# Repeated identity products on TensorE ahead of eight of its waits, in a fused attention and mixture-of-experts layer

## The chip, the cores and the metric

One core of one Trainium2 chip runs the whole layer in one launch. The metric is the device time of a launch in microseconds (us), the median of several. One more execution was taken with the hardware profiler; all rows below are from it, and their times count from the start of its span.

## The reference

The layer takes x of 4 batches by 512 tokens by 512 features and does the following, cut to what matters here:

```
mod = (silu(c) @ wmod) in six parts: sa, ca, ga, sb, cb, gb
h   = layernorm(x) * (1 + ca) + sa
q, k, v = h @ Wq + bq, h @ Wk + bk, h @ Wv + bv     (16 heads of 128)
w   = softmax(q k / sqrt(128) + causal mask)
x   = x + ga * ((w v) @ Wo + bo)
h   = layernorm(x) * (1 + cb) + sb
x   = x + gb * (sum over the top 2 of 8 experts of weight * swiglu(h) + shared swiglu(h))
```

An expert has 352 hidden features; the shared one has 704 and is run as two experts of 352.

## The kernel before

Every large product is made three times: each operand is split into a high part and a low remainder (`_hi`, `_lo`), and `mm3` (L1112) issues hi*hi, hi*lo and lo*hi into one PSUM bank. ScalarE (ACT) copies out of PSUM into the high part, VectorE (DVE) subtracts it to get the low part, and TensorE (PE) waits for that. Each engine has its own program; they are tied by semaphores, and the order within an engine is the order in which the code is written.

**Stage 1** makes q for all batches and heads. TensorE first multiplies out two parts of `mod`, transposes the first batch's normalised x (`transposes`, L1142, called from L1157) and then waits in `q_rows` (L1163) until the modulated rows are split (`hlo_ok`). The banks in use are 2 to 7; bank 1 is first written by the second head.

**Stage 2** is attention, 32 steps of one pair of heads and one batch (`step` in the TensorE program, driven by `walk_steps`). A step multiplies `scores(0)` to `scores(5)` (three parts for each of the two heads, banks 2 and 3), puts the output projection of the step before between them (`project(0)` to `project(3)`), makes the values (`values(0)` to `values(3)`, banks 0 and 1), transposes the softmax blocks (`turn`) and multiplies them with the values (`weigh(0)` into bank 6, `weigh(1)` into bank 7). `scores(i)` waits for the exponentials of part i-2. `weigh(h)` takes three groups g of transposed blocks, each behind a wait for its low part (L1272). The first step has no projection and has all its values first (L1294); the last step (`last`) has no keys for a next step, and does `turn(0)`, `turn(1)`, `weigh(0)`, `weigh(1)` at its end. In the last step DVE's program runs, between the low part of head 0's output (`o_part(0)`) and the low parts of head 1's transposed blocks, the four `c_stats` of a layer norm; ACT copies head 1's blocks only after `weigh(0)` is done.

**Stage 3** is the feed-forward part, 71 jobs of one tile of 128 tokens each (`job`, L1374): 16 jobs of the first shared half, 6 of the second, 39 routed slots and then 10 more of the second shared half. A job multiplies the gate half (`half(..., 0)`), transposes the previous job's hidden rows (`turn_mid`), multiplies the up half (`half(..., 1)`), transposes the next job's tokens (`turn_rows`, which waits for their load) and multiplies the previous job's down projection (`down`). Job 0 comes without a previous one. Between job 0 and job 1 stands a wait for the down weights (L1405), between job 15 and job 16 one for the second shared expert (L1412), job 21 (`R0 - 1`) transposes the first gathered tokens, and the last `down` (L1474) follows its `turn_mid` (L1473).

`ident` (the 128x128 identity) and `causal` (the additive mask block) are in SBUF from the start of the kernel to its end, both of four-byte floats. The `causal` block is added by DVE in `maxima`.

Of the kernel before, what the change touches and what calls it, by code (L numbers as in the profile page):

```python
# [30 lines left out]
P = 128  # L31
# [24 lines left out]
R0 = NT + NB1  # L56
# [70 lines left out]
def adaln_layer(nc, x, wq, bq, wk, bk, wv, bv, wo, bo, gate_t, wexp, c_t, wmod, ident_in, causal_in,  # L127
                tri_in, coef_in, out):
    ctx = ExitStack()
    with ctx:  # L130
# [18 lines left out]
        bank = [ctx.enter_context(nc.psum_tensor(f"bank{i}", [P, T], F32)) for i in range(8)]  # L149


        ident = sbuf(ctx, "ident", [P, P])
        causal = sbuf(ctx, "causal", [P, P])
# [958 lines left out]
        def _(pe):  # L1112
            def mm3(dst, terms):
# [5 lines left out]
                        k += 1  # L1119
                return ins  # L1120

            pe.wait_ge(silu_c, 1)

            def mod_piece(m):
# [10 lines left out]
            def transposes(b, i):  # L1135

                pe.wait_ge(xn_ok, b * TT + (i + 1))
                if not (isinstance(b, int) and b == 0):
                    pe.wait_ge(hf_ok, b * TT + (i - 1))
                for c in range(DC):  # L1140
                    dst = bank[2 + i if isinstance(b, int) and b == 0 else 4 + i % 2]
                    ins = pe.transpose(dst[:, c * P:(c + 1) * P], x_in[:, i, c * P:(c + 1) * P],  # L1142
                                       ident[:, :])
                ins.then_inc(tx_full, 1)
# [10 lines left out]
            ins.then_inc(modt_full, 1)  # L1155
            for i in range(1, TT):
                transposes(0, i)  # L1157

            def q_rows(b, more, first):
                def hidden(h, c):  # L1160
# [53 lines left out]
            def step(p, b, first, last):  # L1214
                n = p * B + b

                def scores(i):

                    h, rows = i // 3, S_PARTS[i % 3]
                    if i % 3 == 0:  # L1220
                        pe.wait_ge(k_ok, n * 2 + (h + 1))
                        pe.wait_ge(q_ok, n * 2 + (h + 1))
                    if not (first and i < 2):
                        pe.wait_ge(s_exp, n * 6 + (i - 1))
                    for r in rows:
                        w = (r + 1) * P
                        at = ROW_AT[r] - ROW_AT[rows[0]]
                        dst = bank[2 + i % 2][:, at:at + w]
                        for k, (a, m) in enumerate(((q_hi, k_hi), (q_hi, k_lo), (q_lo, k_hi))):
                            ins = pe.matmul(dst, a[:, h, r * P:w], m[:, h, 0:w], start=(k == 0), stop=(k == 2))  # L1230
                    ins.then_inc(s_full, 1)

                def values(t):

                    g, i = t // 2, t % 2
                    if i == 0:
                        pe.wait_ge(wv_ok, p + 1)
                        if not first:
                            pe.wait_ge(wo_add, n * TT + (g - 1))
                        else:  # L1240
                            pe.wait_ge(k_ok, g + 1)
                    rows = slice(t * P, (t + 1) * P)
                    ins = mm3(bank[g][:, i * 2 * P:(i + 1) * 2 * P],
                              [(h_hi[:, b * DC + c, rows], h_lo[:, b * DC + c, rows], wv_hi[:, c, :], wv_lo[:, c, :])
                               for c in range(DC)])
                    if i == 1:
                        ins.then_inc(v_full, 1)

                def turn(h, groups):

                    if groups[0] == 0:
                        pe.wait_ge(p_ok, n * 6 + (3 * h + 3))
                    for g in groups:
                        blocks = PT_GROUPS[g]
                        if last and h == 1:
                            if g == 2:
                                pe.wait_ge(v_ok, n * 2 + 1)
                        elif not (first and h == 0 and g < 2):
                            pe.wait_ge(pt_ok, n * 6 + (3 * h + (1 if g == 2 else 0)))
                        for k, at in blocks:  # L1260
                            for r in range(k, TT):
                                ins = pe.transpose(  # L1262
                                    bank[pt_bank(h, g, last)][:, at + (r - k) * P:at + (r - k + 1) * P],
                                    prob[:, h, ROW_AT[r] + k * P:ROW_AT[r] + (k + 1) * P], ident[:, :])
                        ins.then_inc(pt_full, 1)

                def weigh(h):

                    if not first:
                        pe.wait_ge(o_ok, n * 2 + (h - 1))  # L1270
                    for g, blocks in enumerate(PT_GROUPS):
                        pe.wait_ge(pt_ok, n * 6 + (3 * h + g + 1))  # L1272
                        pe.wait_ge(v_ok, n * 2 + (1 if g == 0 else 2))
                        for k, at in blocks:
                            w = (TT - k) * P
                            cols = slice(PT_AT[g] + at, PT_AT[g] + at + w)
                            vals = slice(h * P, (h + 1) * P)
                            for q, (a, m) in enumerate(((v_hi, pt_hi), (v_hi, pt_lo), (v_lo, pt_hi))):
                                ins = pe.matmul(bank[6 + h][:, k * P:T], a[:, k, vals], m[:, cols],  # L1279
                                                start=(k == 0 and q == 0), stop=(g == 2 and q == 2))  # L1280
                    ins.then_inc(o_full, 1)

                def project(i):
                    if not first:
                        free = [(k_ok, n * 2 + 1), (k_ok, n * 2 + 2), (wo_add, n * TT - 3), (wo_add, n * TT - 2)][i]
                        out_tile(n - 1, p if b > 0 else p - 1, i, free)

                def next_keys(h, chunks):
                    if not last:
                        keys(n + 1, p if b < B - 1 else p + 1, (b + 1) % B, h, chunks)  # L1290

                if first:
                    for t in range(TT):
                        values(t)  # L1294
                scores(0)
                scores(1)
                project(0)
                project(1)
                scores(2)
                project(2)  # L1300
                scores(3)
                project(3)
                if not first:
                    values(0)
                scores(4)
                if not first:
                    values(1)
                scores(5)
                if not first:
                    values(2)  # L1310
                    values(3)
                turn(0, (0, 1))
                if last:
                    turn(0, (2,))
                    turn(1, (0, 1, 2))
                    weigh(0)
                    weigh(1)
                    return
                next_keys(0, range(DC))
                turn(0, (2,))  # L1320
                next_keys(1, (0,))
                weigh(0)
                turn(1, (0, 1))
                next_keys(1, range(1, DC - 1))
                turn(1, (2,))
                weigh(1)
                next_keys(1, (DC - 1,))
# [46 lines left out]
            def job(n, s, wofs, prev_ofs, route=False, prev=True, nxt=True, free=None, up_ld=None, prev_at=WD,  # L1374
                    gathered=False):
                half(n, s, wofs, 0, route)
                if up_ld:
                    pe.wait_ge(*up_ld)
                if prev:
                    turn_mid(n - 1, 1 - s)  # L1380
                half(n, s, wofs, 1, route)
                if nxt:
                    turn_rows(n + 1, 1 - s, loaded(n + 1, 1 - s, gathered))
                if prev:
                    down(n - 1, 1 - s, prev_ofs, free, prev_at)
# [16 lines left out]
            pe.wait_ge(g_ok, 1)  # L1402
            pe.wait_ge(we_ld[0], 32)
            job(0, 0, 0, 0, route=True, prev=False, up_ld=(we_ld[1], 32))
            pe.wait_ge(we_ld[2], 32)  # L1405
            job(1, 1, 0, 0, route=True, prev_at=WDA)
            job(2, 0, 0, 0, route=True, prev_at=WDA)
            job(3, 1, 0, 0, route=True, free=(y_gb, 1), prev_at=WDA)
            with pe.Fori(2, NT // 2) as j:
                for k in range(2):  # L1410
                    job(j * 2 + k, k, 0, 0, route=True, free=(y_gb, j * 2 + (k - 2)), prev_at=WDA)
            pe.wait_ge(w_ld[1], 32)  # L1412

            def slot_tokens(c):
# [55 lines left out]
            for n in range(Z0 + 1, NJ):  # L1470
                k = n - Z0
                job(n, n % 2, 0, 0, nxt=n + 1 < NJ, free=(y_ev, NSLOT + k - 2) if k < 3 else (y_gb, R0 + k - 2))
            turn_mid(NJ - 1, (NJ - 1) % 2)  # L1473
            down(NJ - 1, (NJ - 1) % 2, 0, (y_gb, R0 + NB2 - 2))  # L1474


# [648 lines left out]
```

## Time and profile before

| | us |
|---|---|
| median of three runs | 1673.3 |
| lowest, highest | 1672.33, 1673.81 |
| profiled execution, its own time | 1676.7 |
| its span, first to last instruction | 1674.9 |

TensorE is busy 1591.5 us of the span (95%), VectorE 891.5 (53%), ScalarE 697.0 (42%), GpSimd 591.2 (35%). The mean granted TensorE clock is 0.981 of full speed. "PE" is TensorE's multiplying, "PEld" its loading of the stationary operand, which lies beside it. A granted clock of 1.00 is 2.4 GHz and 0.50 is 1.2 GHz.

### The profile page before, as it was taken

To read this page: it belongs to the slowest core of one execution; us is meant where nothing else is said; L and a number is where in the kernel's file an instruction comes from. 1 tells how busy PE (TensorE), PEld (TensorE's weight loads), DVE (VectorE), ACT (ScalarE), POOL (GpSimd) and SP (SyncE) were. 2 spreads that over 40 slices of the span, in tenths; PEclk is the share of its full clock that TensorE was granted. 3 is DMA by queue.
4 is the path that set the end of the run, shared out by engine and by line. 5 is a ranking of instruction groups with operands and counts; after the bars stand their busy time and mean duration, and the time that the engine had idled before them with its cause. 6 is when DMAs were issued, how large, how long until landed. Compare 5 with 4: busy or idle time off the path is not lost.

```text
span 1674.9 us, 29946 instructions
## 1 busy us (share of the span) xinstructions
PE 1591.5 (95%) x9012; PEld 1382.1 (83%) x9013; DVE 891.5 (53%) x2091; ACT 697.0 (42%) x1689; POOL 591.2 (35%) x625
## 2 busy tenths in 40 slices
PE   6999989999999999999999999978998899999997
PEld 3888578888888888888888888767898798888886
DVE  4333136666666566656665666767656322222267
ACT  4222155555555555555555555432231232222332
POOL 0001024544554535444545455655211211111043
PEclk9999999999999999999999999989998999999998
DMA  7522225243343253432423442585213445655455
GB/s 262 200 101 106 95 72 164 64 123 116 111 122 103 72 153 96 129 109 78 152 72 107 118 125 66 164 318 193 88 38 132 151 182 182 252 205 192 178 182 176
DMA packets 178453, 232.40 MB, mean 139 GB/s; under 512 B 78600, under 2 KB 137352, under 8 KB 175328
## 3 DMA queue, kind: packets, MB, share of 16 engines
q1 hardware_dynamic: 168112, 204.74, 37.0%
q0 software_dynamic: 5680, 18.62, 3.9%
q10 hardware_dynamic: 4608, 8.39, 1.6%
q8 instruction: 27, 0.44, 0.1%
q14 instruction: 26, 0.21, 0.0%
HBM read 151.70 MB, written 80.00 MB: 138 GB/s over the span
## 4 chain that ended last, share of the span: by engine, by line
PE 79%; DVE 8%; DMA 6%; ACT 3%; issue 3%; SPq 1%; another core or an unknown queue 0%; POOL 0%; ACTq 0%; DVEq 0%; POOLq 0%
PE bank L1118 48%; PE bank L1195 9%; PE bank L1279 7%; PE bank L1230 7%; DMA slot_results<-y_sb 5%; PE bank L1262 4%; PE bank L1131 1%; PE bank L1336 1%; PE bank L1362 1%; DVE o_lo L1604 1%; DVE pt_lo L1602 1%; ACT prob L939 1%; DVE ht_lo L1778 1%; DMA q_transposed<-q_out 1%; ACT o_hi L972 1%
## 5 line engine op out<-in xcount | busy, mean ns | idle before, releaser
L1118 PE MATMUL bank<-w,xt_hi 128*128 (+2 forms) x1136 | 287.0, 335 | 9.9 <-issue 8.2
L939 ACT ACTIVATE prob<-bank,neg_max 128x128 f32<-128x128 f32 (+3 forms) x256 | 134.0, 526 | 241.3 <-DVE neg_max L1643 238.7
L1118 PEld LDWEIGHTS bank<-w,xt_hi 128*128 128x128 f32 x1136 | 198.7, 191 | 22.0 <-issue 15.5
L680 POOL CAST q_hi<-q_raw 128x512 fp32r<-128x512 f32 x64 | 71.2, 1112 | 386.2 <-PE bank L1230 238.2
L1118 PE MATMUL bank<-w,xt_lo 128*128 (+2 forms) x568 | 185.6, 327 | 0.0
L1118 PE MATMUL bank<-w,ht_hi 128*128 (+3 forms) x426 | 142.6, 416 | 19.2 <-DVE ht_lo L1778 19.2
L1778 DVE TENSOR_TENSOR ht_lo<-bank,ht_hi 128x128 fp32r<-128x128 f32 (+1 forms) x213 | 48.4, 283 | 195.8 <-ACT ht_hi L1052 192.0
L1118 PE MATMUL bank<-wv_hi,h_lo 128*128 128x256 f32 x512 | 144.7, 283 | 0.0
L1118 PE MATMUL bank<-wv_lo,h_hi 128*128 128x256 f32 x512 | 144.5, 282 | 0.0
L1118 PE MATMUL bank<-wv_hi,h_hi 128*128 128x256 f32 x512 | 144.3, 282 | 0.0
L951 ACT ACTIVATE prob<-prob,row_inv 128x128 f32<-128x128 f32 (+3 forms) x256 | 136.2, 556 | 1.4
L1638 DVE TENSOR_REDUCE row_max<-bank 128x1 f32<-128x128 f32 (+3 forms) x256 | 119.8, 489 | 6.6
L682 POOL TENSOR_TENSOR ch_lo<-ch_raw,ch_hi 128x340 fp32r<-128x340 f32 x128 | 117.9, 921 | 10.2
L1602 DVE TENSOR_TENSOR pt_lo<-bank,pt_hi 128x512 fp32r<-128x512 f32 (+1 forms) x192 | 108.4, 592 | 14.8 <-ACT pt_hi L965 14.8
L1604 DVE SCALAR_TENSOR_TENSOR o_lo<-bank,bv_c,o_hi 128x512 fp32r<-128x512 f32 x64 | 48.1, 751 | 116.9 <-ACT o_hi L972 116.9
L1195 PE MATMUL bank<-h_hi,wk_hi 128*128 128x512 f32 x256 | 109.0, 426 | 0.8 <-ACT q_out L900 0.8
L1118 PE MATMUL bank<-h_hi,wq_hi 128*128 128x512 f32 (+1 forms) x256 | 102.3, 400 | 6.9 <-DVE h_lo L1579 6.5
L1118 PEld LDWEIGHTS bank<-w,xt_lo 128*128 128x128 f32 x568 | 108.2, 191 | 0.0
L1602 DVE TENSOR_TENSOR v_lo<-bank,v_hi 128x512 fp32r<-128x512 f32 x64 | 44.3, 692 | 118.2 <-ACT v_hi L958 118.2
L965 ACT ACTIVATE pt_hi<-bank 128x512 fp32r<-128x512 f32 (+1 forms) x192 | 93.3, 525 | 33.2 <-PE bank L1262 32.5
L1118 PEld LDWEIGHTS bank<-w,ht_hi 128*128 128x128 f32 (+1 forms) x426 | 76.8, 193 | 35.9 <-DVE ht_lo L1778 16.8
L900 ACT ACTIVATE q_out<-bank,bq_c 128x512 f32<-128x512 f32 x64 | 43.9, 689 | 143.8 <-PE bank L1118 134.0
(203 smaller groups left out, 4081.6 us busy)
## 6 DMA issues: line engine op xcount, KB each, us to landing
ch_raw<-wexp SPq DMA_DIRECT2D x128, 170.0 KB, 2.6
experts_hi<-ch_hi SPq DMA_DIRECT2D x128, 170.0 KB, 2.0
experts_lo<-ch_lo SPq DMA_DIRECT2D x128, 170.0 KB, 2.1
w<-experts_hi SPq DMA_DIRECT2D x10, 2176.0 KB, 8.4
w<-experts_lo SPq DMA_DIRECT2D x10, 2176.0 KB, 15.0
q_transposed<-q_out SPq DMA_DIRECT2D x64, 256.0 KB, 2.0
q_raw<-q_transposed SPq DMA_DIRECT2D x32, 512.0 KB, 4.2
slot_results<-y_sb SPq DMA_DIRECT2D x39, 256.0 KB
```

Of the source, the lines that this page charges most:

```text
L680: pool.tensor_copy(hi, raw).then_inc(split_hi, 1)
L682: pool.tensor_tensor(lo, raw, hi.bitcast(F32), ALU.subtract).then_inc(done, 1)
L939: ins = act.activation(prob[:, h, ROW_AT[r]:ROW_AT[r] + (r + 1) * P], bank[2 + i % 2][:, at:at + (r + 1) * P], ACT.Exp, bias=neg_max[:, h, ...
L951: ins = act.activation(part, part, ACT.Copy, scale=row_inv[:, h, r:r + 1])
L965: act.activation(pt_hi[:, PT_AT[g]:PT_AT[g] + PT_LEN[g]], bank[pt_bank(h, g, last)][:, 0:PT_LEN[g]], ACT.Copy).then_inc(pt_hi_ok, 1)
L1118: ins = pe.matmul(dst, a, m, start=(k == 0), stop=(k == last))
L1195: ins = pe.matmul(bank[h][:, :], a[:, c, h * P:(h + 1) * P], m[:, b * DC + c, :], start=(c == 0 and k == 0), stop=(c == DC - 1 and k == 2))
L1230: ins = pe.matmul(dst, a[:, h, r * P:w], m[:, h, 0:w], start=(k == 0), stop=(k == 2))
L1262: ins = pe.transpose(bank[pt_bank(h, g, last)][:, at + (r - k) * P:at + (r - k + 1) * P], prob[:, h, ROW_AT[r] + k * P:ROW_AT[r] + (k + 1) ...
L1279: ins = pe.matmul(bank[6 + h][:, k * P:T], a[:, k, vals], m[:, cols], start=(k == 0 and q == 0), stop=(g == 2 and q == 2))
L1602: dve.tensor_tensor(dst, src, hi.bitcast(F32), ALU.subtract).then_inc(done, 1)
L1638: ins = dve.tensor_reduce(row_max[:, h, r:r + 1], bank[2 + i % 2][:, at:at + (r + 1) * P], AX_X, ALU.max)
```

## The change

A helper `spin(b, count)` on TensorE multiplies the identity (stationary) by the causal block (moving) `count` times into the first 128 columns of bank b. Nothing reads the result; it waits on nothing and signals nothing. It is called at eight places, here lettered in program order: A (10 times, before the first wait of `q_rows`), B (4 times, first attention step, between the values and `scores(0)`), C (6 times, last attention step, between `project(1)` and `scores(2)`), D (8 times, last attention step, inside `weigh(0)` before its third group), E (8 times, after job 0), F (6 times, before job 16), G (11 times, in job 21 before the transposes of the first gathered tokens) and H (6 times, before the last `down`).

```diff
@@ tensor program
+            def spin(b, count):
+                for _ in range(count):
+                    pe.matmul(bank[b][:, 0:P], ident[:, :], causal[:, :], start=True, stop=True)
...
             for i in range(1, TT):
                 transposes(0, i)
+            spin(1, 10)
...
                     for g, blocks in enumerate(PT_GROUPS):
+                        if last and h == 0 and g == 2:
+                            spin(1, 8)
                         pe.wait_ge(pt_ok, n * 6 + (3 * h + g + 1))
...
                 if first:
                     for t in range(TT):
                         values(t)
+                    spin(7, 4)
                 scores(0)
                 scores(1)
                 project(0)
                 project(1)
+                if last:
+                    spin(7, 6)
                 scores(2)
...
                 half(n, s, wofs, 1, route)
+                if isinstance(n, int) and n == R0 - 1:
+                    spin(2, 11)
                 if nxt:
                     turn_rows(n + 1, 1 - s, loaded(n + 1, 1 - s, gathered))
...
             job(0, 0, 0, 0, route=True, prev=False, up_ld=(we_ld[1], 32))
+            spin(4, 8)
             pe.wait_ge(we_ld[2], 32)
...
                     job(j * 2 + k, k, 0, 0, route=True, free=(y_gb, j * 2 + (k - 2)), prev_at=WDA)
+            spin(7, 6)
             pe.wait_ge(w_ld[1], 32)
...
             turn_mid(NJ - 1, (NJ - 1) % 2)
+            spin(0, 6)
             down(NJ - 1, (NJ - 1) % 2, 0, (y_gb, R0 + NB2 - 2))
```

## Rows read from the trace of the kernel before

**Rows 1.** The page: busy time of the engine; shares of the last-ending chain by engine.
```profile
PE 1591.5 (95%) x9012; PEld 1382.1 (83%) x9013; DVE 891.5 (53%) x2091; ACT 697.0 (42%) x1689; POOL 591.2 (35%) x625
...
PE 79%; DVE 8%; DMA 6%; ACT 3%; issue 3%; SPq 1%; another core or an unknown queue 0%; POOL 0%; ACTq 0%; DVEq 0%; POOLq 0%
```

**Rows 2.** Stretches: length, PE, PEld, DVE, ACT, POOL busy, clock, DMA share, GB/s.
```profile
20.61:27.06 6.45, 0.00 (x1) 0.01 (x1) 5.02 (x6) 6.45 (x16) 0.00 (x0) 0.71 0.71 253
27.06:30.10 3.04, 3.04 (x7) 2.46 (x8) 2.07 (x1) 3.04 (x3) 0.00 (x0) 0.50 0.16 60
238.19:248.56 10.37, 6.67 (x25) 5.15 (x25) 7.39 (x26) 7.44 (x22) 3.90 (x4) 0.67 0.22 51
1081.69:1088.24 6.55, 4.67 (x19) 4.12 (x19) 6.04 (x10) 1.07 (x2) 2.89 (x5) 0.74 0.83 249
1092.29:1095.97 3.68, 0.01 (x2) 0.00 (x1) 3.54 (x9) 0.96 (x5) 2.46 (x3) 0.88 1.04 390
1095.97:1101.90 5.93, 5.93 (x17) 4.97 (x18) 3.48 (x9) 2.71 (x7) 5.85 (x7) 0.50 0.49 145
1110.93:1116.59 5.66, 3.45 (x24) 3.12 (x24) 2.37 (x5) 2.73 (x6) 0.47 (x1) 1.00 0.96 333
1116.59:1121.25 4.66, 0.00 (x0) 0.03 (x1) 3.82 (x7) 2.05 (x4) 0.00 (x0) 0.75 1.05 409
1121.25:1125.78 4.53, 4.53 (x16) 4.04 (x16) 1.28 (x7) 0.57 (x1) 3.14 (x7) 0.50 1.03 418
1136.84:1140.97 4.13, 0.00 (x1) 0.03 (x1) 4.06 (x8) 0.60 (x1) 0.20 (x1) 0.81 0.88 312
1140.97:1146.26 5.29, 5.29 (x19) 5.20 (x20) 2.32 (x5) 1.14 (x5) 0.00 (x0) 0.50 1.07 388
1161.84:1168.20 6.36, 3.36 (x18) 2.96 (x18) 4.90 (x9) 0.60 (x1) 6.12 (x6) 1.00 0.16 44
1316.63:1322.84 6.21, 0.00 (x1) 0.00 (x1) 0.52 (x1) 0.00 (x0) 0.52 (x2) 0.80 1.05 447
1322.84:1327.16 4.32, 4.32 (x12) 3.55 (x13) 0.69 (x1) 0.60 (x1) 1.10 (x2) 0.50 0.86 329
1662.71:1666.06 3.35, 0.00 (x1) 0.00 (x0) 3.19 (x7) 0.60 (x3) 0.00 (x0) 0.86 0.17 64
1666.06:1670.30 4.24, 4.21 (x9) 2.81 (x9) 0.00 (x0) 0.00 (x0) 0.00 (x0) 0.50 0.03 12
```

**Rows 3.** Timeline of TensorE after job 16: start, length, engine, line, operation, operands, count.
```profile
1259.59 0.38 PE L1430 MATMUL bank<-hot,tri 128*128 128x128 f32 x2
1259.81 0.39 PE L1431 MATMUL bank<-hot,ones 128*128 128x128 f32 x2
```

**Rows 4.** Timeline around place D, from weigh(0)'s third group on; idle before in brackets.
```profile
1116.02 0.33 PE L1279 MATMUL bank<-pt_hi,v_hi 128*128 128x256 f32 x1
...
1116.71 0.69 ACT L972 ACTIVATE o_hi<-bank,bv_c 128x512 fp32r<-128x512 f32 x1 [2.71 <-PE bank L1279]
...
1117.43 0.75 DVE L1604 SCALAR_TENSOR_TENSOR o_lo<-bank,bv_c,o_hi 128x512 fp32r<-128x512 f32 x1 [2.98 <-ACT o_hi L972]
...
1118.10 2.46 DVE L1740 BATCH_NORM_STATS2 stat<-acc 128x6 f32<-128x512 f32 x4
1120.48 1.27 DVE L1602 TENSOR_TENSOR pt_lo<-bank,pt_hi 128x512 fp32r<-128x512 f32 x2
```

**Rows 5.** Stretches after place D, and the seven jobs before F, as in Rows 2.
```profile
1125.93:1140.97 15.04, 10.07 (x53) 8.89 (x53) 14.53 (x19) 3.12 (x5) 10.07 (x8) 0.95 0.62 239
...
1204.00:1251.60 47.60, 46.98 (x278) 43.69 (x278) 23.41 (x61) 15.54 (x46) 9.08 (x7) 1.00 0.16 47
```

**Rows 6.** Timeline around place B: last product of scores(0), then DVE's mask.
```profile
237.39 0.28 PE L1230 MATMUL bank<-k_hi,q_lo 128*128 128x256 f32 x1
...
238.26 0.42 DVE L1634 TENSOR_TENSOR bank<-bank,causal 128x256 f32<-128x256 f32 x1
```

**Rows 7.** Timeline around place F: the first product of job 16, and the next wait.
```profile
1251.59 0.49 PE L1118 MATMUL bank<-w,xt_hi 128*128 128x352 f32 x2
...
1257.40 0.73 PE L1118 MATMUL bank<-w,ht_hi 128*128 128x512 f32 x2 [0.98 <-DVE ht_lo L1778]
```

## The prediction

> **What bounds the kernel now.** I read the page's busy shares and the chain that ended last first: TensorE is busy 95% of the span and makes up 79% of the chain [rows 1]. So a product that is added on TensorE costs its full time unless it lies in one of TensorE's waits, and a product that is made faster gives its time back. I then went through the span for stretches in which the granted clock is below 1.00, and laid them beside TensorE's waits in the timeline. The clock goes to 0.50 nine times, each time after TensorE has waited, and comes back some microseconds after the work resumed. Eight of the nine stand in [rows 2]: those at places A to E, G and H, and the one from 1081.69 for comparison. While it is at 0.50 (1.2 GHz) TensorE is busy all the time in the rows after the waits (5.93 of 5.93 us, 5.29 of 5.29), so each microsecond at 0.50 has half a microsecond of loss in it. That is what the added products can win: work in a wait, so that the clock is not lowered.
>
> Added work in a wait keeps the clock up only if little of the wait is left. What little means has to come from this trace. The six waits of 3.35 us and more were all followed by 0.50. The ones between 1.8 and 3.1 us went both ways: the stretch from 1081.69 holds a wait of 6.55 - 4.67 = 1.88 us and fell, the one from 238.19 begins with 2.35 us and fell (10.37 - 6.67 = 3.70 us idle in all), the one from 1110.93 holds 5.66 - 3.45 = 2.21 and stayed at 1.00, the one from 1161.84 holds 6.36 - 3.36 = 3.00 and stayed at 1.00 [rows 2]. Two of four. So the length does not decide alone, and I give a wait cut down to 1.8 to 3.1 us an even chance of holding the clock, and a longer one none.
>
> The Trainium skill ("TensorE: Matmul & The Clock Gate", Part 1: The HAM clock gate) says that the moment at which the clock switches is not tied to the kernel and differs from run to run of the same code. By that rule a wait of middling length falls in some executions and not in others; the trace agrees in that 3.00 us stayed and 1.88 fell. The sum does not use it.
>
> **What one added product costs.** The kernel has the same form already, four-byte 128x128 by 128x128: L1430 and L1431 show two passes each, and start 1259.81 - 1259.59 = 0.22 us apart [rows 3]. So 0.22 us at full clock, and twice that, 0.44, at 0.50. 4, 6, 8, 10 and 11 of them are 0.88, 1.32, 1.76, 2.20 and 2.42 us; all 59 are 13.0 us of busy time.
>
> The skill's figure for a sustained stream of loads and products at 128 columns ("TensorE: Matmul & The Clock Gate", Back-to-back issue gap) is 81 ns. Were it that, ten would fill 0.8 us, less would be left hidden, and the three uncovered places below would cost 18 x 0.081 = 1.5 us at most. The row is for two passes of four-byte data and decides.
>
> **The places, one by one.**
>
> A (10). The wait from 20.61 is 6.45 us and hides 2.20; 4.25 are left, more than any wait that kept the clock. Cost 0, gain 0 (were the clock held, 3.04 / 2 = 1.5).
>
> G (11). The wait for the gathered tokens is 6.21 us and ends with a transfer, which TensorE doesn't move; 2.42 are hidden, 3.79 are left. Cost 0, gain 0 (at most 4.32 / 2 = 2.2) [rows 2].
>
> C (6). Wait 3.68, hidden 1.32, left 2.36. If the clock holds, 5.93 us at 0.50 become 2.97: gain 2.97, even chance.
>
> E (8). Wait 4.13, hidden 1.76, left 2.37. The wait belongs to DVE, busy 4.06 of it. Gain 5.29 / 2 = 2.65, even chance.
>
> H (6). Wait 3.35, hidden 1.32, left 2.03. The nine products of the last down projection take 4.24 us at 0.50; gain 2.12, even chance, and it is the end of the kernel, with nothing beside it [rows 2].
>
> B (4). There is no wait here: the products stand between the values and scores(0), and TensorE's wait of 2.35 us comes after scores(0) and scores(1). They push scores(0)'s end from 237.67 (237.39 + 0.28) to 238.55; DVE began its mask at 238.26, when it had done the values, so 0.88 turns into 0.3 us on the softmax chain, at most 0.88 [rows 6]. TensorE's wait after it shrinks by 0.5 to 1.8, but the stretch has 1.35 us more idle in two further waits for ACT, and is set by ACT and DVE; I take a gain of 0.3, bounds 0 and half of the time at 0.50 that TensorE works, about 2.7.
>
> D (8). No wait either: the third group of weigh(0) started at 1116.02 behind the second without a pause. Its end releases ACT's o_hi (idle 2.71 before it, for TensorE), that DVE's o_lo (idle 2.98, for ACT), then come the four statistics and pt_lo, for which weigh(1) waits until 1121.25 [rows 4]. All of this moves by 1.76, and TensorE's wait of 4.66 keeps its length, so the clock falls as before. Behind it DVE is busy 14.53 of the 15.04 us up to job 1, and from there TensorE nearly without a break (46.98 of 47.60) [rows 5]: nothing absorbs it. Cost 1.76; from below 1.2, if DVE's half microsecond of idle gives; from above 3.5, if it ran at 0.50. Gain 0 (at most 4.53 / 2 = 2.3, if the shifted wait happened to hold the clock).
>
> F (6). No wait: job 16 followed without a pause at 1251.59. But at 1257.40 TensorE waits 0.98 us for DVE, whose routing work doesn't depend on it. 1.32 - 0.98 = 0.34 are left, bounds 0.3 and 1.32 [rows 7]. No clock was lost here.
>
> **Sum.** Costs 0.3 + 1.76 + 0.34 = 2.4. Gains: half of (2.97 + 2.65 + 2.12) is 3.9, and 0.3 for B, 4.2. Since in other executions than the profiled one a wait of the kernel before may also have kept its clock, less is there to win on a median; I take 3.7. Net -1.3. The profiled execution took 1676.7 (span 1674.9 and 1.8 around it) and would come to 1675.4; it was 3.4 above the median of the runs, so on the median 1673.3 - 1.3 = 1672.0.
>
> **Rivals.** What a measurement of this kernel can tell from no change is about 0.2%, 3.35 us: faster is below 1669.95, slower above 1676.65.
>
> 1. The clock holds at C, E and H each time. For it: what is left is 2.03 to 2.37 us, under the 3.00 that held it. Against: 1.88 and 2.35 fell. Gain 7.74 less costs 2.4: -5.3, 1668.0; with a part at A or G 1666.
>
> 2. The clock falls everywhere all the same: the added products are hidden or paid for and don't do what they are there for, because whatever is left of the wait is enough. For it: the two that fell. The costs remain, +2.4, 1675.7, still within 0.2%.
>
> 3. Slower: the uncovered products at B, D and F are what decides. 18 x 0.22 = 3.96 us, if neither DVE's lead at B nor its lag at F takes a part, with no clock saved: 1677.3. It decides from the point at which more than 3.35 us of the 3.96 show and nothing is won at C, E and H. For it: three of eight places have no wait at all. Against: the cover at B and F can be read in the rows.
>
> **Chances.** Forecast (some hold, some fall) 0.45; rival 1 0.22; rival 2 0.20; rival 3 0.10; 0.03 for a gain beyond rival 1. Faster 0.22 + 0.03 = 0.25, slower 0.10, same 0.65. The forecast's own range is 1670 to 1674.5. The range that holds 8 in 10 reaches into rivals 1 and 2 to 1668.0 and 1676.2.
>
> **What would show it.** In the changed kernel's trace: the clock at 0.50 after A, D and G as before, a mix after C, E, H; weigh(0) to weigh(1) with the same wait of about 4.7 us but 1.8 later; the softmax wait after B shorter by 0.5; at F the wait of 0.98 gone. It would be wrong if a product of this form took much else than 0.22 us, if the clock held after A or G, or if the weights of D's successors were what job 1 waits for, so that D's delay vanished.

## The result, and the profile after

In its first measurement the changed kernel is slower. Over 20 runs of each on one chip its median is 1678.78 us and that of the kernel before 1674.97 (1670.16 to 1680.24); the ratio is 1.0026, 95% interval 1.0015 to 1.0037, so +4.4 us (+2.5 to +6.2). Two later measurements gave +0.7 and +1.8 us with zero inside the interval. The prediction was 1672.0, that is -1.3 us, no measurable change. The profiled execution took 1680.47 us, span 1678.6, against 1676.7 and 1674.9. The page of the changed kernel, busy time by engine, then the chain by engine:

```profile
PE 1604.9 (96%) x9130; PEld 1396.2 (83%) x9131; DVE 890.5 (53%) x2091; ACT 697.5 (42%) x1689; POOL 590.0 (35%) x625
...
PE 82%; DVE 7%; DMA 4%; ACT 3%; issue 3%; another core or an unknown queue 0%; SPq 0%; POOL 0%; ACTq 0%; DVEq 0%; POOLq 0%
```

TensorE has 118 more records, two for each of the 59 products, and 13.4 us more of busy time; 13.0 were forecast. DMA's and VectorE's shares of the chain go down [rows 1], as one would expect where parts of waits for them are now products. The mean granted clock rose only from 0.981 to 0.984.

The stretches of the changed kernel that answer to [rows 2], same columns (length, five engines' busy time, clock, DMA share, GB/s). In order, each wait with what follows it: A's, D's, E's, the one in job 3, the one for the gathered tokens, H's.

```profile
22.59:26.82 4.23, 0.00 (x1) 0.01 (x1) 2.78 (x5) 4.23 (x10) 0.00 (x0) 0.89 0.64 205
26.82:32.72 5.90, 5.90 (x14) 4.64 (x15) 4.93 (x3) 4.85 (x4) 0.00 (x0) 0.50 0.34 87
...
1114.82:1119.48 4.66, 0.00 (x1) 0.03 (x1) 3.83 (x7) 2.05 (x4) 0.00 (x0) 0.86 1.06 398
1119.48:1124.30 4.82, 4.71 (x16) 4.02 (x16) 1.42 (x8) 0.76 (x2) 3.43 (x7) 0.50 1.05 418
1138.47:1140.28 1.81, 0.01 (x2) 0.03 (x1) 1.81 (x4) 0.00 (x0) 0.00 (x0) 1.00 0.36 137
1140.28:1145.00 4.72, 4.72 (x32) 4.68 (x32) 3.16 (x8) 1.03 (x5) 0.00 (x0) 1.00 1.08 381
1158.74:1161.74 3.00, 0.00 (x1) 0.01 (x1) 2.96 (x6) 0.60 (x1) 3.00 (x3) 1.00 0.27 87
1161.74:1165.92 4.18, 4.18 (x12) 3.48 (x13) 1.56 (x3) 0.00 (x0) 2.96 (x3) 0.59 0.00 0
1318.17:1324.34 6.17, 0.00 (x0) 0.00 (x1) 0.52 (x1) 0.00 (x0) 0.51 (x2) 0.89 1.00 426
1324.34:1329.80 5.46, 5.46 (x16) 4.59 (x17) 0.69 (x1) 1.07 (x2) 1.10 (x2) 0.50 0.73 297
1669.68:1671.69 2.01, 0.00 (x1) 0.00 (x0) 1.92 (x5) 0.00 (x0) 0.00 (x0) 1.00 0.28 105
1671.69:1674.10 2.41, 2.35 (x9) 1.61 (x9) 0.02 (x1) 0.00 (x0) 0.00 (x0) 1.00 0.06 21
```

The rows to compare with before: E and H held the clock (1.00 after waits of 1.81 and 2.01 us), A and D did not, and two rows contradict what I wrote. The gathered-token wait is still 6.17 us long: the eleven products of G are not in it. And the 3.00 us in job 3, which kept the clock in [rows 2], were this time followed by 0.59, the mean of 4.18 us of which 3.4 stood at 0.50.

Where G's products stand, in the timeline of the changed kernel (start, length, engine, line, operation, count):

```profile
1299.84 0.49 PE L1372 MATMUL bank<-ident,h_mid 128*128 128x128 f32 x3
...
1302.11 2.62 PE L1124 MATMUL bank<-causal,ident 128*128 128x128 f32 x22
...
1304.56 0.60 PE L1346 MATMUL bank<-ident,xin 128*128 128x128 f32 x4
...
1324.34 0.90 PE L1346 MATMUL bank<-ident,xin 128*128 128x128 f32 x3 [6.17 <-DMA xin<-ffn_rows,slot_tokens]
```

And the same place in the kernel before, where the transposes of job 22's tokens start with no wait in front:

```profile
1302.84 0.33 PE L1118 MATMUL bank<-w,xt_lo 128*128 128x352 f32 x1
1303.01 0.60 PE L1336 MATMUL bank<-ident,xin 128*128 128x128 f32 x4
```

The wait of 6.21 us at 1316.63 in [rows 2] stands two jobs later, in job 23. In job 21 the 2.62 us are bare: nothing in the kernel waits there that they could hide in.

D went as forecast. The changed kernel around weigh(0)'s third group, columns as in [rows 4]:

```profile
1112.46 2.00 PE L1124 MATMUL bank<-causal,ident 128*128 128x128 f32 x16
1114.22 0.36 PE L1286 MATMUL bank<-pt_hi,v_hi 128*128 128x256 f32 x1
...
1114.93 0.69 ACT L972 ACTIVATE o_hi<-bank,bv_c 128x512 fp32r<-128x512 f32 x1 [5.81 <-PE bank L1286]
...
1115.65 0.75 DVE L1619 SCALAR_TENSOR_TENSOR o_lo<-bank,bv_c,o_hi 128x512 fp32r<-128x512 f32 x1 [6.07 <-ACT o_hi L972]
...
1119.48 0.77 PE L1286 MATMUL bank<-pt_hi,v_hi 128*128 128x512 f32 x1 [4.66 <-issue]
```

ACT's idle time ahead of o_hi grew from 2.71 to 5.81 us and DVE's from 2.98 to 6.07, while TensorE's own wait is 4.66 us as before: the products only moved it. Of the 3.1 us more, 1.8 are the products. Most of the rest is a stretch at 0.50 from 1107.9 to 1111.3, behind the wait of 2.2 us before the last block of turn(0), which in [rows 2] (from 1110.93) had kept the clock. No product was added there either.

### The profile page after: what moved, and what is told of

It reads as the page before. It is cut to its first block, busy times and chain, and to the rows that moved or that the text cites. A ratio compares the mean times of both kernels' runs of the same rounds, so it can differ in the third digit from the quotient of the medians.

```text
span 1678.6 us, 30182 instructions
## 1 busy us (share of the span) xinstructions
PE 1604.9 (96%) x9130; PEld 1396.2 (83%) x9131; DVE 890.5 (53%) x2091; ACT 697.5 (42%) x1689; POOL 590.0 (35%) x625
## 4 chain that ended last, share of the span: by engine, by line
PE 82%; DVE 7%; DMA 4%; ACT 3%; issue 3%; another core or an unknown queue 0%; SPq 0%; POOL 0%; ACTq 0%; DVEq 0%; POOLq 0%
PE bank L1118 50%; PE bank L1200 9%; PE bank L1286 7%; PE bank L1235 7%; PE bank L1267 4%; DMA slot_results<-y_sb 4%; PE bank L1135 1%; PE bank L1346 1%; PE bank L1372 1%; DVE pt_lo L1617 1%; DVE o_lo L1619 1%; ACT o_hi L972 1%; ACT prob L939 1%; DVE ht_lo L1793 1%; DVE row_max L1653 1%
## 5 line engine op out<-in xcount | busy, mean ns | idle before, releaser
L1118 PEld LDWEIGHTS bank<-w,ht_hi 128*128 128x128 f32 (+1 forms) x426 | 76.9, 194 | 33.0 <-DVE ht_lo L1793 13.6
```

The lines of the kernel that those rows point to most:

```text
L1118: ins = pe.matmul(dst, a, m, start=(k == 0), stop=(k == last))
```

## The experiments

All ratios are against the kernel before on the same chip in the same session. In the three sessions the kernel before had medians of 1670.09 (20 runs), 1673.26 (23) and 1670.54 us (23), with mean clocks of 0.983, 0.983 and 0.984. A difference in us is the ratio's, times the median of the kernel before; it can differ a little from the difference of the two medians. Diffs are against the changed kernel, if nothing else is said.

| kernel | session | median us | ratio, 95% | mean clock |
|---|---|---|---|---|
| changed kernel, first measurement | | 1678.78 | 1.0026, 1.0015 to 1.0037 | 0.985 |
| uncovered | 1 | 1674.85 | 1.0026, 1.0012 to 1.0040 | 0.984 |
| covered | 1 | 1665.24 | 0.9975, 0.9956 to 0.9994 | 0.988 |
| uncovered4 | 1 | 1692.63 | 1.0133, 1.0112 to 1.0155 | 0.986 |
| fill | 1 | 1658.99 | 0.9929, 0.9912 to 0.9946 | 0.998 |
| after_again (changed kernel) | 2 | 1672.96 | 1.0004, 0.9993 to 1.0016 | 0.988 |
| g_moved | 2 | 1673.12 | 0.9994, 0.9984 to 1.0005 | 0.987 |
| fill_half | 2 | 1665.04 | 0.9957, 0.9943 to 0.9972 | 0.993 |
| after_third (changed kernel) | 3 | 1671.62 | 1.0011, 0.9996 to 1.0027 | 0.987 |
| covered_again | 3 | 1667.88 | 0.9987, 0.9972 to 1.0002 | 0.986 |
| fill2 | 3 | 1659.14 | 0.9936, 0.9920 to 0.9951 | 0.998 |

My theory after the result: the uncovered products (B, D, F, and G as well) cost more than the covered ones (A, C, E, H) give. The rival: the costs are as predicted, and the covered ones cost something by themselves.

**uncovered**: B, D, F and G alone.

```diff
-            spin(1, 10)            # A; and C, E and H likewise
```

> Only B (4), D (8), F (6) and G (11). Theory 1 (the wait that G was meant for stands two jobs later, in job 23; at job 21 TensorE goes through without a pause, so G costs its full 11 x 0.215 us): B 0.3 + D 1.7 + F 0.3 + G 2.4 = +4.7 us over the kernel before, and the clock falls where it did. Theory 2 (G is hidden, as predicted): +2.4. Theory 3 (the slowdown isn't the products' own time but the routed stage, whose waits for slot_results stores happened to be longer): within 1 us of the kernel before.

Measured +4.3 us (+2.0 to +6.7). So these four by themselves make a loss of the size first measured for the whole.

**covered**: A, C, E and H alone.

```diff
-                    spin(7, 4)     # B; and D, F and G likewise
```

> Only A (10), C (6), E (8) and H (6), which stand in waits. Theory 1 (as predicted, they cost nothing and keep the clock up in about half of the executions): -2 to -4 us. Theory 2 (they hold the clock each time): -7. Theory 3 (they do not matter to the clock): 0, and then the whole change is the cost of the uncovered ones.

Measured -4.2 us (-7.3 to -1.0): work in these waits alone makes the kernel faster. The rival falls. Together the two halves make +0.1 us, where the whole had measured +4.4; so the first measurement of the whole is not simply their sum, and it was repeated.

**uncovered4**: B, D, F and G with four times the count.

```diff
-                            spin(1, 8)
+                            spin(1, 32)     # D; B 16, F 24, G 44
```

> B, D, F and G with four times the products (16, 32, 24, 44), to lift their cost well out of the noise. At 0.215 us each: B 3.4 less DVE's lead of 0.6 = 2.9, D 6.9, F 5.2 less DVE's lag of 1.0 = 4.2, G 9.5. Theory 1 (G in full): +23.4 us. Theory 2 (G hidden in a wait of 6.2 us): +17 or less. If D's delay is absorbed behind it: +16.

Measured +22.2 us (+18.7 to +25.9). In its timeline G's 44 products and the transposes behind them:

```profile
1307.77 9.99 PE L1124 MATMUL bank<-causal,ident 128*128 128x128 f32 x88
1317.59 0.60 PE L1343 MATMUL bank<-ident,xin 128*128 128x128 f32 x4
```

The interval from job 21's `turn_mid` to job 22's is 6.72 us in all three profiles of the kernel before, 9.16 in the changed one (+2.44 for 11) and +9.82 here for 44: 0.22 us a product, none of it hidden.

**fill**: nine waits of the kernel, among them D's and G's true ones, filled nearly to their ends.

```diff
-            spin(1, 10)
+            spin(1, 26)                    # A; C 15, E 17, H 13
...
+                if first:
+                    spin(7, 9)             # before scores(2), for B
...
+                    spin(1, 20)            # last step, between weigh(0) and weigh(1), for D
...
+                if isinstance(n, int) and n == R0 + 1:
+                    spin(2, 25)            # job 23, for G
...
+                if isinstance(n, int) and n == 3:
+                    spin(6, 12)
+                if isinstance(n, int) and n == NT + 2:
+                    spin(6, 13)            # before down in jobs 3 and 18
```

> None of the uncovered places; the products stand in nine waits read from the timeline and nearly fill them: A 26, 9 before the first step's scores(2), C 15, 20 between weigh(0) and weigh(1) of the last step, E 17, 12 before the down projection in job 3, 13 before that in job 18, 25 before the transposes of job 23, H 13. Theory 1 (a wait that is nearly filled keeps the clock at 2.4 GHz every time): the clock falls at one place at most, and -8 to -14 us. Theory 2 (the products don't count for the clock): the clock falls at nine places as before, 0 us, with up to +2 where a wait turns out shorter than its filling. Theory 3 (half of the waits hold): -4 to -7.

Measured -11.9 us (-14.7 to -9.0). The same stretches as above, in fill: A; the last attention step; E; job 18 and after; the gathered tokens.

```profile
20.20:26.90 6.70, 6.15 (x56) 5.96 (x53) 5.32 (x7) 6.70 (x17) 0.00 (x0) 1.00 0.71 256
1109.00:1124.00 15.00, 12.50 (x89) 11.52 (x90) 9.94 (x22) 4.82 (x10) 5.80 (x10) 1.00 1.01 375
1134.00:1142.00 8.00, 6.77 (x49) 6.57 (x49) 6.40 (x13) 1.02 (x5) 0.00 (x0) 1.00 0.99 357
1264.00:1282.00 18.00, 17.68 (x124) 16.66 (x123) 15.88 (x29) 2.15 (x6) 3.13 (x2) 1.00 0.16 58
1300.00:1324.00 24.00, 23.25 (x155) 21.94 (x155) 5.18 (x12) 4.96 (x15) 5.69 (x9) 1.00 0.64 252
```

The clock is 1.00 in each. It stood at 0.50 for 3.4 us in two other stretches, from 244.9 in the first attention step (place B) and from 1084.6, behind a wait of 1.90 us that no product fills; one at most was expected. C's 15 products filled its wait and did not overrun it, since TensorE still waited 0.16 us for the exponentials behind them. So C's wait was about 3.5 us long in this execution:

```profile
1090.86 1.67 DVE L1779 SCALAR_TENSOR_TENSOR h<-h,rstd,mods 128x512 f32<-128x512 f32 x1
...
1091.97 3.51 PE L1124 MATMUL bank<-causal,ident 128*128 128x128 f32 x30
1095.65 0.50 PE L1235 MATMUL bank<-k_hi,q_hi 128*128 128x512 f32 x1 [0.16 <-ACT prob L939]
```

**after_again**: the changed kernel once more, no edit.

> The changed kernel unaltered, on the chip of the next ones. Theory 1 (its parts add up: uncovered +4.4, covered -4.2, with their intervals): between 0 and +4 us. If its first ratio of 1.0026 is what it is worth: +4.4 us.

Measured +0.7 us (-1.2 to +2.7), beside +2.5 to +6.2 the first time. The intervals barely touch, and executions and chip were others, so which of these made the size differ is not shown.

**g_moved**: the changed kernel with G in job 23.

```diff
-                if isinstance(n, int) and n == R0 - 1:
+                if isinstance(n, int) and n == R0 + 1:
                     spin(2, 11)
```

> The changed kernel with G's 11 products not in job 21 but two jobs later, in job 23, where TensorE waits 6.2 us for gathered tokens. Theory 1 (G stood where there is no wait): 2.4 us less than the changed kernel, and TensorE goes through job 21 without the 2.4 us. Theory 2 (the place makes no difference): as the changed kernel.

Job 22's transposes, then G's products and job 24's transposes in its timeline:

```profile
1306.70 0.60 PE L1346 MATMUL bank<-ident,xin 128*128 128x128 f32 x4
...
1313.41 2.62 PE L1124 MATMUL bank<-causal,ident 128*128 128x128 f32 x22
...
1320.07 0.66 PE L1346 MATMUL bank<-ident,xin 128*128 128x128 f32 x4 [4.05 <-DMA xin<-ffn_rows,slot_tokens]
```

The interval from job 21 to job 22 is back at 6.72 us, and the wait is 4.05 instead of 6.17. So the 2.44 us are G's placing, shown in the trace. The whole kernel's time does not show them: the ratio is 0.9994 (0.9984 to 1.0005) against 1.0004 (0.9993 to 1.0016) for the changed kernel beside it, intervals that overlap, and the medians are 1673.12 and 1672.96 us.

**fill_half**: fill with half of each count; the diff is against fill.

```diff
-            spin(1, 26)
+            spin(1, 13)     # B 5, C 8, D 10, E 9, job 3 6, job 18 7, G 13, H 7
```

> The nine places of the kernel that fills the waits, each with half of its products (13, 5, 8, 10, 9, 6, 7, 13, 7), so that about half of each wait is left idle. Theory 1 (what is left of a wait decides, and between 1.8 and 3 us it goes either way): about half of the full filling's gain, -4 to -8 us. Theory 2 (any work in a wait keeps the clock): as the full filling, -12. Theory 3 (only a filled wait helps): 0 to -2.

Measured -7.2 us (-9.5 to -4.7), clock 0.993, between fill and the kernel before. In its profile the clock fell at three of the nine places (B, D and job 23) and held at six: a half-filled wait holds the clock in part of the cases.

**before_again** and **before_third**: the kernel before, one profile each.

> The kernel before once more, for a second profile. If TensorE's wait of 3.68 us before the last step's scores(2), on which C's gain was reckoned, is what that step always has, it is there again. If it came from slow VectorE rows in that one execution, it is about 1.3 us, as in the profile with only the uncovered places.

> The kernel before, for a third profile: the waits at A, D, E, H and in jobs 3, 18 and 23 as long as in the other two, within 0.3 us; the one at C between 1.3 and 1.9 us, not 3.68.

They took 1671.06 and 1679.19 us (spans 1669.2 and 1677.4, clocks 0.984 and 0.979). Around C, the first profile of the kernel before:

```profile
1089.41 2.98 POOL L704 TENSOR_TENSOR acc<-acc,mods 128x512 f32<-128x512 f32 x2 [0.74 <-DMA mods<-mod_rows]
1089.73 1.52 DVE L1758 SCALAR_TENSOR_TENSOR h<-acc,mean_var,mods 128x512 f32<-128x512 f32 x1
1091.29 1.66 DVE L1761 SCALAR_TENSOR_TENSOR h<-h,rstd,mods 128x512 f32<-128x512 f32 x1
1095.97 0.80 PE L1230 MATMUL bank<-k_hi,q_hi 128*128 128x512 f32 x1 [3.67 <-ACT prob L939]
```

and before_again:

```profile
1088.15 0.79 DVE L1758 SCALAR_TENSOR_TENSOR h<-acc,mean_var,mods 128x512 f32<-128x512 f32 x1
...
1092.48 0.50 PE L1230 MATMUL bank<-k_hi,q_hi 128*128 128x512 f32 x1 [1.86 <-ACT prob L939]
```

The layer norm's rows on DVE took 1.52 and 1.66 us beside GpSimd's L704 once, and 0.79 when they missed it. The wait behind them was 3.67 us in the first profile, 1.86 and 2.08 in the other two, where 1.3 and 1.3 to 1.9 had been expected. Of all fourteen profiles only fill's had one as long again, also with a slow DVE row beside L704. The changed kernel has none left:

```profile
1091.90 0.40 PE L1118 MATMUL bank<-wo_hi,o_lo 128*128 128x512 f32 x1
1092.13 1.50 PE L1124 MATMUL bank<-causal,ident 128*128 128x128 f32 x12
1093.57 0.50 PE L1235 MATMUL bank<-k_hi,q_hi 128*128 128x512 f32 x1
```

**after_third**: the changed kernel, a third measurement, no edit.

> The changed kernel unaltered, a third time. So far +0.26% (0.15 to 0.37) and +0.04% (-0.07 to 0.16). Theory 1 (costs of 4.7 us in the uncovered places against 4 us won in the covered ones, and what differs between the two is which executions and which chip): between 0 and +3 us. Theory 2 (the first is what it is worth): +4.4.

Measured +1.8 us (-0.7 to +4.5). With the profiles of all runs one can look at the 3.00 us wait in job 3, which none of these kernels but the three fills touches. TensorE's product right behind it, in covered, then in after_third:

```profile
1159.68 0.73 PE L1118 MATMUL bank<-w,ht_hi 128*128 128x512 f32 x2 [3.00 <-DVE ht_lo L1787]
```

```profile
1163.05 1.22 PE L1118 MATMUL bank<-w,ht_hi 128*128 128x512 f32 x2 [3.00 <-DVE ht_lo L1793]
```

The wait is the same to a hundredth; one execution went on at full clock (0.73 us for the pair) and one at half (1.22). The clock kept 1.00 there in seven profiles of seven without the whole change (three of the kernel before, two of covered, two of the uncovered kernels), and fell in four of four with it (three of the changed kernel, g_moved). The way from job 3 to job 4 is 10.04 us in the kernel before and 1.54, 1.53, 2.60 and 1.54 us more in those four.

**covered_again**: covered, a second measurement.

> Only A, C, E and H again, since its interval was wide (-0.44% to -0.06%). Theory 1: -3 to -5 us. If the parts don't add up to the whole, it is nearer to 0.

Measured -2.2 us (-4.7 to +0.3). The direction is the same, but the gain is smaller than the -3 to -5 expected, and this interval alone would not show it.

**fill2**: fill with C at 7 and nine products before the third block of the last step's `turn(0)`; the diff is against fill.

```diff
-                    spin(7, 15)
+                    spin(7, 7)
...
+                    spin(7, 9)      # before the third block of turn(0)
```

> The kernel that fills nine waits, with C cut from 15 to 7 products, because C's wait is 1.3 to 1.9 us in all profiles but the first, and with 9 more in the wait of 2.2 us before the last step's turn(0, (2,)). Theory 1 (C's 15 overran its wait by 1.4 us): 1 to 2 us faster than the first filling, so -13 to -14 us against the kernel before. Theory 2 (C's overrun was hidden): as the first filling, -11 to -12.

Measured -10.7 us (-13.4 to -8.2); its profiled execution:

```profile
core 0: 1655.3 us, clock 0.998
```

Not to be told from fill: theory 2 held, and not the 1 to 2 us more of theory 1. Fill's profile has no overrun at C that could have been won back. Both beat the kernel before and the changed one.

## Why the prediction was wrong, point by point

**G is the step that failed.** "The wait for the gathered tokens is 6.21 us and ends with a transfer, which TensorE doesn't move; 2.42 are hidden, 3.79 are left. Cost 0, gain 0": the size and the cause of the wait were right, the job was not. I took the row with the gathered tokens' releaser for the transposes of the job that the diff names, and didn't count jobs up to it: `turn_rows` in job 21 transposes job 22's tokens, and the row at 1322.84 belongs to job 24's. Cost 2.44 us instead of 0, the same in three profiles of the changed kernel, gone in g_moved's. With it rival 3 would have been "four of eight places", 29 x 0.22 = 6.4 us uncovered at most instead of 3.96, and the forecast about +1.

**C: a wait sized from one execution.** I gave it half of 2.97. The 3.68 us were a meeting of DVE's rows with L704; 1.9 and 2.1 us stand in the other two profiles of the kernel before. The clock fell behind C's wait in two of these three (for 6.8 us, and for 3.4 in before_third) and in none of the changed kernel's three. From the last step's scores(0) to its turn(0) it took 21.85, 17.18 and 18.98 us before and 16.6 in each of the changed ones. But uncovered, without a product at C, took 16.66 too and kept its clock there, so this difference can't be put down to C. What C won is open. I enter 0; its upper bound is what the falls cost the kernel before, 2.7, 0 and 1.6 us (13.92, 11.20 and 12.77 us from scores(2) to turn(0)), 1.4 on the mean.

**D right.** Forecast 1.76. The start of weigh(1) behind it moved by 1.8 us against the start of weigh(0), by 2.2 where weigh(0) began at 0.50; its wait stayed at 4.66, and the clock fell. **B right**: `scores(0)` moved by 0.81, the way to the end of the step shortened by 0.45, cost 0.4 for 0.3; its TensorE wait is 1.81 for 2.35. No clock was gained there. **F**: +1.34 at job 16, 1.25 of it back by job 17, because the wait of 0.98 us and a little more is gone; 0.07 for 0.34. **A right**: 4.23 us of wait left and 0.50 after it. **The price** per product was right, 0.22: the twenty passes at A took 2.40 us in the trace, G's 22 took 2.62.

**E a bit less.** The clock held in two of six profiles with these products, where 1.78 and 1.81 us of wait were left, and fell for 3.4 us in four, where 2.15 to 2.58 were left; the kernel before has 6.8 us at 0.50 each time. That is not far from the half that was given. From the start of weigh(1) to job 2's `turn_mid`, 30.96 us before, the six had -1.34, -0.86, +0.57, -1.31, -0.85 and -0.86, a mean of -0.8 instead of -1.3. **H more.** It held in five of six, in all three of the changed kernel: from the last `turn_mid` to the end of TensorE's last product 8.05 us became 6.19, a gain of 1.86 of 2.12, where I had counted half.

**"An even chance" was the wrong form.** I treated a wait of 1.8 to 3.1 us as an independent draw in each execution. Job 3 shows otherwise: one wait, 3.00 us each time, no edit near it, seven of seven against four of four. That cost the changed kernel 1.54, 1.53 and 2.60 us in its three profiles, 1.9 on the mean, which stood in no term. The traces show what differed. All changes of the clock in one profile lie a whole number of equal steps apart, so from the falls one can count on to where such a moment comes in job 3. In the seven profiles that kept the clock it came 1.45 to 1.76 us into the wait, near its middle; in the four that lost it, at 0.38, 1.13, 1.93 and 0.49 us (the changed kernel's three, then g_moved). H reads alike: the five that held had the moment 1.29 to 1.64 us into its 2.01 us, and in g_moved, which fell, it came after the wait's end. So where the wait lies against these moments goes with the outcome, and work added elsewhere can shift it. No run moved job 3 alone, so that it decides is read from eleven profiles and not tested; nor is it shown why the seven agree so closely while the changed kernel's three do not. The Trainium skill ("TensorE: Matmul & The Clock Gate", Part 1, What's actually happening) says of the clock gate that it runs by itself and isn't restarted by the kernel. The traces agree: the three profiles of the changed kernel have three different offsets at the same wait. My reading of the same wait as kept, from a single profile, could not see that.

The prediction's count of waits also left out one of the nine stretches at 0.50 that it had found: the longest inside the kernel, 10.24 us behind a wait of 3.25 us in job 18.

**The sum again, with measured terms.** Costs B 0.4, D 2.0, F 0.1, G 2.4, job 3 1.9: 6.8. Gains E 0.8, H 1.9: 2.7. Net +4.1 instead of -1.3, or +2.7 if C had its 1.4. Of the 5.4 between the two G is 2.4, job 3 1.9 and C's half 1.5; E takes 0.5 more and H gives 0.8 back, the rest is small. Measured were +4.4, +0.7 and +1.8 us, so the sum is in the upper part of what was measured and does not explain the lower two.

**What stays open** is the spread of these three. One part can be read: the wait of 3.2 us in job 18, which no edit but the fills touches. The clock fell behind it in all profiles that leave it unfilled, but stayed at 0.50 for 10.2 us in the three of the kernel before, for 13.6 in the first of the changed kernel, and for 3.4 in after_again and after_third. From job 18's `turn_mid` to job 21's that makes 32.01 us, 32.99, and 28.84 and 28.67. The stretches of the changed kernel's first profile, and of after_third:

```profile
1271.76:1285.40 13.64, 12.45 (x43) 11.50 (x44) 7.63 (x11) 1.07 (x4) 1.71 (x1) 0.50 0.01 5
```

```profile
1274.60:1278.04 3.44, 3.13 (x7) 2.48 (x8) 2.41 (x5) 0.00 (x0) 0.00 (x0) 0.50 0.00 1
1278.04:1288.24 10.20, 10.20 (x71) 9.66 (x69) 7.97 (x13) 1.56 (x5) 1.74 (x1) 1.00 0.00 0
```

The same 13.64 us hold 43 products in the one and 78 in the other. So two executions of one kernel differ here by 4.2 us, about the whole effect. How often each outcome comes in the unprofiled runs isn't known. Further differences of the profiled pair stand in the routed jobs: from job 63 to 64, for instance, the kernel before took 8.46, 8.45 and 6.73 us in its three profiles and the changed one 11.54, 8.43 and 6.72, and no product was added near it. The 11.54 hold a wait of 3.02 us with 3.4 us at 0.50 behind it.

The other rivals: rival 1 was right for H alone; rival 2's arithmetic, costs and no gain, would have been near had its costs held G. The measured 1.0026 is 1677.7 on the median shown, above my range, whose upper end took G for free.

## What to carry to other kernels

Before work is put into a wait, find the wait by its job and step in the timeline, instruction by instruction, and read it in more than one profile: a releaser's name shows what was waited for, not which turn of the loop. Filler on the critical engine costs its whole length beside the wait (2.4 us here), and in it gives back one or two microseconds if the clock holds. Added work can also cost a clock that was kept at a wait far from it (1.5 to 2.6 us in job 3). If a clock is worth keeping, fill the wait nearly to its end and fill all of them: 0.998 and -0.6 to -0.7%, where half filling gave -0.4% and the changed kernel's eight places +0.0 to +0.3%.

## What the runs showed of the hardware

- At these waits of 1.8 to 3.3 us the length alone did not decide: 3.00 us in job 3 held in seven profiles and fell in four; 3.2 us in job 18 fell in all eleven that leave it unfilled; 2.01 us at H held in five and fell in one. At job 3 and H the outcome went with how far into the wait the next possible change of the clock came.
- Falls once begun lasted 3.4, 6.8, 10.2 or 13.6 us. In job 18 the kernel before stayed at 0.50 for 10.24 us in which TensorE had no idle time at all (16 products of 40 columns each take 3.4 us of it). Being busy in the profile is not enough to get the clock back at once.
- Products whose result nobody reads hold the clock: 0.983 became 0.998. From that rise alone 0.015 x 1670 = 25 us were to be had, and 12 arrived; part of the time at 0.50 lies in waits, where it costs nothing.
- DVE's 128x512 rows of two tensors took 1.52 and 1.66 us beside GpSimd's two-tensor L704 and 0.79 apart from it. The Trainium skill ("GPSIMD Engine Reference", 1. Specifications) names contention with VectorE's instructions of two SBUF inputs; these rows agree.
